# Two-layer graph network on one Trainium2 core: source matches stored with 128 partitions and loaded by SyncE's queue

## What is computed

```
# layer 0 (edge_attr_16)
msg = relu(h[src] + edge_attr_16 @ W_edge.T + b_edge)
agg = segment_sum(msg, dst, 6250)
y   = relu(batchnorm((h + agg) @ W1.T + b1)) @ W2.T + b2
x   = x + y
# layer 1 (edge_attr_64)
msg = relu(concat(h[src], edge_attr_64) @ M_W.T + M_b)
agg = segment_sum(msg, dst, 6250)
x   = x + relu(concat(h, agg) @ U_W.T + U_b)
```

## Time and profile before

| what | value |
|---|---|
| time, median of 3 runs | 4725.73 us |
| the 3 runs | 4706.73, 4725.73, 4726.61 us |
| the profiled execution's own time | 4710.86 us |
| its span | 4709.1 us |
| granted TensorE clock, mean | 0.674 of full speed |
| busy: TensorE matmul / weight load | 2550.8 / 2122.0 us |
| busy: GpSimd / VectorE / ScalarE | 2087.7 / 1516.1 / 960.1 us |
| mean DMA rate | 120 GB/s |
| one turn of layer 0, from GpSimd's starts at 2003.49 and 2100.84 | 97.4 us |
| one turn of layer 1, from its starts at 4010.67 and 4047.88 | 37.2 us |

### The profile page before, as it was taken

One profiled execution on the slowest core, in us unless ns is written; L12 is line 12 of the kernel. 1 busy time (PEld: TensorE's weight loads), 2 busy tenths in 40 slices (PEclk: granted clock), 3 DMA queues, 4 the chain that ended last, 5 costly groups with the idle time before them and its releaser, 6 DMA issues. The chain is left out here.

```text
span 4709.1 us, 73575 instructions
## 1 busy us (share of the span) xinstructions
PE 2550.8 (54%) x25733; PEld 2122.0 (45%) x25733; DVE 1516.1 (32%) x2605; ACT 960.1 (20%) x2153; POOL 2087.7 (44%) x2185
## 2 busy tenths in 40 slices
PE   3455545655466554655456554554655555554554
PEld 3354445544355443545345444554544444443443
DVE  4332223322233222322223222332444434433443
ACT  1321112221122211212122111222321111111111
POOL 5344453445434454344544445344243443344343
PEclk9766666666666666666667666676667766676776
DMA  6554434544345443554445444442355554555551
GB/s 187 140 139 124 113 105 120 143 121 115 105 120 143 125 110 104 132 143 117 109 112 140 130 113 109 126 125 76 95 120 124 123 123 111 122 123 124 112 128 51
DMA packets 703632, 565.17 MB, mean 120 GB/s; under 512 B 491942, under 2 KB 605748, under 8 KB 699042
## 3 DMA queue, kind: packets, MB, share of 16 engines
q1 hardware_dynamic: 625244, 402.10, 34.2%
q0 software_dynamic: 69440, 107.94, 8.8%
q10 hardware_dynamic: 8736, 51.91, 3.2%
HBM read 294.89 MB, written 266.88 MB: 119 GB/s over the span
## 5 line engine op out<-in xcount | busy, mean ns | idle before, releaser
L1200 PE MATMUL ps_w<-arena 128*64 128x128 f32 (+1 forms) x9040 | 1199.4, 313 | 992.0 <-issue 900.2
L737 POOL DMA_INDIRECT edge_store<-side,slot_idx x1054 | 1019.3, 967 | 1562.3 <-issue 1270.7
L759 POOL DMA_INDIRECT gathered_rows<-node_table_l,plain_slot x1116 | 1060.6, 950 | 967.9 <-DVE arena L1623 589.9
L1200 PEld LDWEIGHTS ps_w<-arena 128*64 128x64 f32 x9040 | 901.5, 165 | 1186.4 <-issue 1066.9
L1600 DVE TENSOR_TENSOR arena<-ps_c,dst_rel 128x1024 f32<-128x1024 f32 (+1 forms) x476 | 526.1, 1105 | 1109.4 <-remote 828.4
L1135 PE MATMUL ps_p<-w_both,side 80*128 80x128 f32 x3228 | 652.7, 362 | 417.6 <-issue 193.7
L912 ACT ACTIVATE arena<-arena 128x512 f32<-128x512 f32 (+1 forms) x616 | 366.2, 595 | 2354.0 <-remote 856.2
L1135 PEld LDWEIGHTS ps_p<-w_both,side 80*128 80x128 f32 x3228 | 566.9, 262 | 465.1 <-issue 332.8
L1609 DVE TENSOR_TENSOR arena<-ps_r,arena 128x512 f32<-128x512 f32 (+1 forms) x476 | 299.4, 629 | 579.4 <-remote 559.2
L1585 DVE TENSOR_SCALAR arena<-arena,iota_p 125x512 bf16<-125x512 bf16 (+1 forms) x442 | 146.3, 349 | 961.0 <-ACT arena L899 662.6
L1188 PE MATMUL ps_r<-tab,arena 125*128 125x64 bf16 x5100 | 281.8, 212 | 252.3 <-DVE arena L1585 166.9
(11 more groups left out here) (124 smaller groups left out, 1024.9 us busy)
## 6 DMA issues: line engine op xcount, KB each, us to landing
edge_store<-zeros SPq DMA_DIRECT2D x34, 3300.0 KB
arena<-edge_store SPq DMA_DIRECT2D x34, 1650.0 KB, 10.8
src_store<-arena SPq DMA_DIRECT2D x204, 250.0 KB
side<-attr SPq DMA_DIRECT2D x172, 256.0 KB
arena<-edge_store SPq DMA_DIRECT2D x34, 1056.0 KB
arena<-edge_store SPq DMA_DIRECT2D x34, 594.0 KB
plain_store<-plain_e SPq DMA_DIRECT2D x35, 512.0 KB
side<-plain_store SPq DMA_DIRECT2D x35, 512.0 KB
```

Source lines behind the costliest of these rows:

```text
L737: pool.indirect_dma_start(out=store, in_=stage[:, c, i, :], in_offset=None, out_offset=bass.IndirectOffsetOnAxis(ap=slot_idx[:, s, t + i:t ...
L759: pool.indirect_dma_start(out=rows[s][:, i, :], out_offset=None, in_=table[layer], in_offset=bass.IndirectOffsetOnAxis(ap=plain_slot[:, s, ...
L1200: mm = pe.matmul(ps_sum[layer][t % 2][:, 0:width], msg[:, slot, t, :], dst_match[:, slot, t, 0:width], start=(first and t <= layer), stop= ...
```

## The change

`src_store` gets 128 partitions instead of 125, and both the stores in layer 0 and the loads in layer 1 move 128 of them. Partitions 125 to 127 hold whatever stands there, and TensorE still reads partitions 0 to 124 alone. In layer 1, `load_src_part` is issued by SyncE directly behind the part of edge rows of the same group, and ScalarE's own function for it, with its semaphore increment, is gone; with that, three of ScalarE's last turns can lie in its loop, which changes none of its instructions' order.

```diff
--- before.py
+++ after.py
@@ -217,7 +217,7 @@
     store = nc.dram_tensor("edge_store", (NB * GROUP_ROWS, ROW), F32, kind="Internal").ap()
     store_groups = store.rearrange("(g r) c -> g r c", r=GROUP_ROWS)
     plain_store = nc.dram_tensor("plain_store", (PARTS, P, PLAIN * D), F32, kind="Internal").ap()
-    src_store = nc.dram_tensor("src_store", (NB, NODE_P, NODE_COLS * P), BF16, kind="Internal").ap()
+    src_store = nc.dram_tensor("src_store", (NB, P, NODE_COLS * P), BF16, kind="Internal").ap()
     with ExitStack() as ctx:
         def sb(name, shape, dt=F32):
             return ctx.enter_context(nc.sbuf_tensor(name, shape, dt))
@@ -321,7 +321,7 @@
         plain_l1 = [cols(side, nodes_cols + i * plain_cols, plain_cols) for i in range(2)]
         plain_part = [[plain_e[:, 0, :, :]] * 2, [by_tile(v) for v in plain_l1]]
 
-        src_l1 = [v.bitcast(BF16) for v in (ranking[0:NODE_P, 0:NODE_COLS * P // 2], cols(side, 0, NODE_COLS * P // 2, NODE_P))]
+        src_l1 = [v.bitcast(BF16) for v in (ranking[:, 0:NODE_COLS * P // 2], cols(side, 0, NODE_COLS * P // 2))]
 
         edge = [cols(arena, s * e_cols, e_cols).rearrange("p (j r) -> p j r", r=HALF_ROW) for s in range(2)]
         at = 2 * e_cols
@@ -396,7 +396,6 @@
         pool_released = sem("pool_released")
         pe_released = sem("pe_released")
         sp_released = sem("sp_released")
-        act_released = sem("act_released")
         landed = [sem(f"landed{c}") for c in range(len(CHUNKS))]
         plain_idx_landed = [sem(f"plain_idx_landed{s}") for s in range(2)]
         bcast_done = sem("bcast_done")
@@ -546,7 +545,7 @@
                 sp.wait_ge(src_matched, halves(g, min(2 * u + 1, NH - 1)))
                 sp.sem_inc(sp_released, 1)
                 sp.dma_start(src_store[bass.ds(g, 1), :, j * P:(j + nt) * P].rearrange("a p e -> (a p) e"),
-                             src_match[0:NODE_P, slot, :, :].rearrange("p h e -> p (h e)")[:, 0:nt * P]).then_inc(src_stored[slot], 16)
+                             src_match[:, slot, :, :].rearrange("p h e -> p (h e)")[:, 0:nt * P]).then_inc(src_stored[slot], 16)
 
             def load_src_part(g, p, k):
                 j, nj = LOAD_PARTS[k]
@@ -696,6 +695,7 @@
                     sp.wait_ge(dense_sems[1].rows_used, units(m, u) + 2)
                     sp.sem_inc(sp_released, 1)
                     load_edges_part(m + 2, s, k)
+                    load_src_part(m + 2, s, k)
 
             def next_plain(m, s):
                 sp.wait_ge(dense_sems[1].plain_used, plain_units(m, NV - 1))
@@ -911,12 +911,6 @@
                 act.wait_ge(d.scattered, step + 1)
                 act.activation(msg[:, slot, 0:nt, :], pre[:, slot, 0:nt, :], ACT.Relu).then_inc(d.relu_done, 1)
 
-            def load_src_part(g, p, k):
-
-                j, nj = LOAD_PARTS[k]
-                act.dma_start(src_l1[p][:, j * P:(j + nj) * P], src_store[bass.ds(g, 1), :, j * P:(j + nj) * P]
-                              .rearrange("a p e -> (a p) e")).then_inc(src_landed[p][k], 16)
-
             def begin(layer):
                 read_meta(layer, 0, 0, 0)
                 if layer == 0:
@@ -937,8 +931,6 @@
                             middle(1, NG - 1)
                     act.wait_ge(dense_sems[layer].rows_used, units(0, u) + 2)
                     relu(layer, u, u % 2, nt)
-                    if layer == 1 and u in (LOAD_UNITS - 1, NU - 1):
-                        load_src_part(2, 0, u // LOAD_UNITS)
                 read_meta(layer, 1, 0, 1)
                 if layer == 0:
                     for i in range(2):
@@ -960,9 +952,6 @@
                             copy_spread(m + 1, p, i)
                     act.wait_ge(d.rows_used, units(m + 1, u) + 2)
                     relu(layer, at + u, (par + u) % 2, nt)
-                    if layer == 1 and u in (LOAD_UNITS - 1, NU - 1) and not (isinstance(m, int) and m + 3 >= NB):
-                        act.sem_inc(act_released, 1)
-                        load_src_part(m + 3, p, u // LOAD_UNITS)
                     if more and 2 <= u < 6:
                         evacuate(m + AHEAD, 1 - s, 2 * u - 4)
                         evacuate(m + AHEAD, 1 - s, 2 * u - 3)
@@ -1074,11 +1063,10 @@
             first_group(1)
             for s in range(2):
                 dense_turn(1, 0, s, first=s == 0)
-            with act.Fori(1, (NB - 4) // 2) as n:
+            with act.Fori(1, (NB - 2) // 2) as n:
                 for s in range(2):
                     dense_turn(1, n, s)
-            for m in range(NB - 4, NB - 1):
-                dense_turn(1, m // 2, m % 2, last=m == NB - 2)
+            dense_turn(1, (NB - 2) // 2, 0, last=True)
             more = general_flag(act)
             for m in range(NB - 1, PARTS):
                 last_plain(1, m)
@@ -1183,7 +1171,7 @@
                     pe.wait_ge(d.rows_used, units(g, u))
                 for t in range(nt):
                     to = (i % 2 * HALF + t) * D
-                    match = src_match[0:NODE_P, slot, i % 2, t * P:(t + 1) * P] if layer == 0 else src_l1[p][:, (j + t) * P:(j + t + 1) * P]
+                    match = src_match[0:NODE_P, slot, i % 2, t * P:(t + 1) * P] if layer == 0 else src_l1[p][0:NODE_P, (j + t) * P:(j + t + 1) * P]
                     for k in range(3):
                         last = pe.matmul(ps_r[slot][:, to:to + D], match, tab[:, j + t, k, :], start=(k == 0), stop=(k == 2))
                 if i % 2 == 1 or i == NH - 1:
```

## The result

| | before | changed |
|---|---|---|
| median, us | 4705.77 (20 runs, 4681.85 to 4729.02) | 4685.84 (20 runs, 4666.59 to 4713.85) |
| profiled execution, us | 4710.86 | 4691.88 |
| first to last plain unit of layer 1, us | 1178.2 | 1171.5 |
| that first plain unit, us | 3501.8 | 3489.4 |

The account below looks back on a forecast made before the run. The prediction took a turn to be GpSimd's issuing time, with TensorE starved, plus about 14 us of VectorE and TensorE work. Terms of 0 and -5 us for stores, from a 4717.5 us mean, gave 4713 us; range 4615 to 4745 us.

Parts of the forecast that it names:

- no change to tell: Whole kernel: median within 0.5% of the kernel before, 4702 to 4749 us, with 4690 to 4740 as its own range; 0.62.
- Step 1: Both layers: a turn is GpSimd's issuing time, with TensorE starved whatever the DMA load, plus a stretch of about 14 us.
- ScalarE's issues and SyncE's queue: Layer 1: ScalarE loses 64 issues, SyncE gains 64, 17 us each; waits and 18.7 us of index slack cover them: 0.
- The loads land earlier: Layer 1: loads of matches and edge rows land some 10 us earlier, with nobody named as waiting: 0.
- The stores: Layer 0: 238 stores take 1.4 us less each; gain between 0 and 333 us, taken as 5 us.
- The sum: Whole kernel: the terms add to -5 us, set against a mean of 4717.5 us, giving 4713 us.
- Rival A: Before `match_src`: VectorE's 36 "issue" waits are landings of stores, each 1.4 us shorter; 50 us faster, 4663 us; 0.13.
- Rival B: Layer 1: five engines' load delays TensorE's supply; 93 us faster, 4620 us; 0.13, including similar gains from better spread load.
- Rival C: Layer 1: SyncE's queue becomes the bound, indices go out late; 91 us slower, 4804 us; 0.12.

Follow-up runs that it names:

- e6: Kernel before, but GpSimd gathers 4 of 8 tiles per plain unit in layer 1; 4306.0 us, ratio 0.9151 where the kernel before takes 4698.53 us.
- x1: The changed kernel, unchanged, on a chip where the kernel before takes 3059.8 us; 2904.22 us, ratio 0.9496.
- e1: Kernel before with 128 partitions for stores and loads, ScalarE still issuing the loads; 2906.91 us, ratio 0.9489 where the kernel before takes 3062 us.
- x2: e1 again: 128 partitions with ScalarE issuing the loads, against the kernel before at 3059.8 us; 2905.33 us, ratio 0.9495.
- x3: e2 again: 125 partitions with SyncE issuing the loads, against the kernel before at 3059.8 us; 3089.88 us, ratio 1.0107.
- e5: Kernel before with stores of 128 partitions, loads still 125 and issued by ScalarE; 4692.26 us, ratio 0.9988 where the kernel before takes 4698.53 us.
- r1: The kernel before, unchanged, run once for a trace on the chip where it takes 4698.53 us; 4717.21 us.
- r2: The changed kernel, unchanged, on the chip where the kernel before takes 4698.53 us; 4686.89 us, ratio 0.9972.
- e3: Kernel before with six of seven stores per group in layer 0 writing one column of matches; 3089.71 us, ratio 1.0089 where the kernel before takes 3062 us.
- e2: Changed kernel put back to 125 partitions, SyncE issuing the loads; 3095.31 us, ratio 1.0104 against the kernel before at 3062 us.
- e4: Kernel before plus a second, unread transfer of each group's matches on the same five engines; 3432.66 us, ratio 1.1207 where the kernel before takes 3062 us.

## Why the prediction was right, point by point

- **The range and "no change" held, its own bounds in us did not.** Forecast 4713 us and "no change to tell" (0.62); measured 4685.84 against 4705.77. The prediction's own last sentence calls it wrong if the median leaves 4702 to 4749, and 4685.84 does; it also lies under the 4690 to 4740 given for no change. Those bounds were 0.5% on either side of the kernel before's first median, 4725.7. Around the 4705.77 of 20 runs they are 4682 and 4729, and 4685.84 is inside by 4 us. So "no change" is right as a ratio (0.9967) and was close to failing. Part of the 27 us between forecast and median is no effect of the change: the kernel before itself came out 12 us under the 4717.5 that the sum started from.
- **Step 1, TensorE is starved while GpSimd issues, whatever the DMA load.** Right for this chip. With the DMA share of the stretch halved (0.57 to 0.27), 23 matmuls became 24; with half the gathers (e6) the turn lost 11.0 us where GpSimd's half lost 10.0. But it was told as a property of the kernel, and it is not one: x1 and e1 have no such stretch. That the result came from a chip of this kind was luck, since nothing in the prediction asked for it: at 3060 us the same change gives 5.1%, outside the 2.3% that the range allowed.
- **ScalarE's issues and SyncE's queue: 0.** Right as far as the rows show. The indices had 18.7 us of slack and now have about 30. On a 3060 us chip, x1 against x2 gives 0 too. At 4700 us the move was never measured without the 128 partitions, nor they without it: x2 and x3 were meant to do that and fell on another chip.
- **The loads land earlier: 0.** Perhaps a little too small; not shown. In both pairs layer 1 became shorter (6.7 us of 1178.2; 10.8 of 1180.9), 0.2 to 0.3 us per turn, but e5, with the loads of the kernel before, is 6.2 us shorter than r1 too. The prediction had "nobody is named as waiting"; GpSimd's idle time before its gathers put down to VectorE fell from 589.9 to 572.8 us, with the DMA share from 3600 to 4500 falling from 0.54 to 0.49. Which transfer makes room for what, if any, stays open: e5 and r2 differ by less than their intervals.
- **The stores: -5 us of 0 to -333.** Small, as taken. The stretch before layer 1 was shorter by 12 us in the first pair and 44 in the second, too far apart to be one number, and by 35 us in e6 against r1, where nothing in layer 0 differs; e5, which has all of the stores' part, measured 0.9988 with 1 in its interval. The upper bound was far off: it takes each store as waited for, and the rows name two such waits before and one after. It also counts the 34 short stores (62.5 KB) at the price of the long ones; 204 x 1.4 + 34 x 0.35 is 297 us. Even at 3060 us, where VectorE waits for 63 stores, layer 0 gained nothing.
- **The sum.** -5 us, measured -15.5 (-9 to -22): the terms taken as 0 and 5 were too small by some 10 us in all, and no run tells which of them.
- **Rival A** (the "issue" waits before L1585 are landings of stores, 50 us): wrong. They went from 287.4 us in 36 places to 300.7 in 39. e3 speaks against it for a 3060 us chip.
- **Rival B** (five engines delay TensorE's supply, 93 us): its sign, more matmuls beside the gathers, did not come (2302 in all of layer 1 before, 2196 after). Its price was also too high: it took the turn of 37.2 us as the usual one, and the mean is 34.7, 0.4 us above the 34.3 that it was to shrink to. The prediction gave it weight for a rule of the Trainium skill (Runtime: NRT & Kernel Launch, "Instruction fetch mechanics"), that each sequencer fetches its instructions by DMA. x1 and the result's profile both moved 180 packets in the queue that fetches instructions, so the amount fetched through that queue is not what differs between a starved TensorE and one that isn't.
- **Rival C** (SyncE's queue becomes the bound): wrong for the change, right for half of it. e2 and x3 show its mechanism, place and releaser as described, at a price of 30 to 33 us over the kernel before and 186 over the changed one (x3 against x1).
- **What the prediction could not see.** The five engines needed about 25 us of a turn (e2: 25.8 us, of which 12.5 are the matches by the prediction's rate; the rest must be what they carry of edge rows and plain messages). In a turn of 34.7 us on average that is hidden; where nothing starves TensorE, it is the bound, and the change moves the bound to GpSimd's 20.0 us. This is argued from e2, e4 and the gain of e1, since the kernel before itself has no trace from such a chip. An estimate of its turn there: e4's layer 1 takes 1181.4 us, less the 370 that the copies added 811, or 24 us for each of 34 turns. The rule of the Trainium skill on 5 engines for 125 and 16 for 128 (DMA: Bandwidth & Descriptors, "Why a DMA increments its semaphore by 16 and not by 1") agrees with the trace: with 128 partitions the matches alone take 98.9% of 16 engines in e1, and with 125 they run on 4.8.

## What to carry to other kernels

Put a price on a narrow transfer (few DMA engines) as time per turn, and compare it with the turn that is left when the present bound goes, not only with the present turn: here about 25 us lay hidden under 34.7 and stood bare over 20. If a queue is to take over a wide load, widen the load first; the move alone cost 1%, and with 128 partitions it cost nothing. And where a trace has long idle time put down to "issue", measure on a second chip before you call the change worthless.

## What the runs showed of the hardware

- One program, one core, two times: 4698.53 and 4705.77 us on two occasions, 3062.29 and 3059.8 on two chips. The changed kernel shows the same pair, 4685.84 and 2904.22. In its two profiles the granted clock differs, 0.674 against 0.808, but the mean matmul of L1188 only by 4% (312 and 301 ns); the 980 us of "issue" idle time before one line of matmuls compare with 1782 us between the two times. At 4700 us TensorE crawls while GpSimd issues indirect DMAs: in layer 1 of the kernel before it starts 3.6 matmuls per us beside them and 13.1 in GpSimd's pauses (in layer 0 2.8 and 7.8), and in x1, with GpSimd issuing all the time, 13.7 and 7.8. What in the chip or its setting makes this so is not settled: no run changed it, and nothing in the two profiles names it.
- One SyncE issue of a load on five engines held its sequencer for a median of 10.9 to 11.1 us (e2), the same load over 128 partitions for 4.8 to 4.9 (x1), with small issues of 0.3 us otherwise: some 2.3 times as long on 5 engines as on 16. On the result's chip the 128-partition loads held it for 3.4 to 3.6.
